# Two wide VectorE instructions per group of edges issued as four narrow ones each, in a graph kernel

## Chip, cores and metric

One NeuronCore of a Trainium2 chip runs the whole program. The metric is the device time in microseconds of one execution. Before the change it is 4437.84 us, the median of 3 runs (4432.64 to 4450.03).

## What is computed

Four layers work on a graph of 3125 nodes with 96 features and 100000 edges that are sorted by their target. Each layer normalizes its input, applies ReLU and adds its result to `x`. The change touches the last two layers:

```python
# message layer
msg  = relu(x[src] + edge_attr_96)                   # 100000 x 96
h    = x + segment_sum(msg, dst)                     # 3125 x 96
out  = x + relu(relu(h @ W1 + b1) @ W2 + b2)

# gate layer
edge_input = concatenate([x[src], edge_attr_32])     # 100000 x 128
messages   = gelu(edge_input @ mW1 + mb1) @ mW2 + mb2
gates      = sigmoid(gelu(edge_input @ gW1 + gb1) @ gW2 + gb2)
aggregated = segment_sum(messages * gates, dst)
update     = gelu(concatenate([x, aggregated]) @ uW1 + ub1) @ uW2 + ub2
out        = layernorm(x + update) * ln_g + ln_b
```

The two layers before them (a power iteration and three graph convolutions) use dense count matrices and are not touched.

## The kernel before

The edges are cut into 98 groups (`NG`) of 8 tiles (`GT`) of 128 edges, one edge on each partition. Both layers loop over these groups, and each engine has a queue of its own for the loop. Tables of node rows lie in HBM: `h_rows` (96 columns) for the message layer, `first_rows` (192 columns: the node's share of the message's and of the gate's first product) for the gate layer.

**Message layer.** POOL gathers the rows of a group by eight indirect DMAs of 128 rows (L777) into a ring of 7 slots (`RING`), after a wait that the slot's group is done (`group_done`, L774). SP loads the edges' features of the group into a second ring (L762). DVE then does, for each group, in this order: the add of rows and edges, 768 columns on 128 partitions, both inputs and the output in SBUF (L815, `added`); a one-hot matrix of edges against the 64 nodes of a step (L824, 512 columns); a wait for PE; the add of the step's sum to `aggT` (L828, 64 columns, one input in PSUM); and `group_done` (L829). ACT applies ReLU to the sum of rows and edges (L792), and PE multiplies rows by one-hot, 8 products into one PSUM tile (L865, `step_summed`). DVE waits for that sum before it goes on to the next group, so the steps of one group are a chain: L815, L792, L865, L828.

**Gate layer.** POOL gathers 192 columns a row (L981) into a ring of 7, after a wait for `rows_used`, which ACT raises with its second activation of the group (L1002). PE multiplies the edges' 32 features by the weights in two halves of four tiles (L1150, `edge_mixed`), and DVE adds each half from PSUM to the gathered rows (L1048, `added`). ACT applies Gelu to the gate's half (L999, into `gated`) and to the message's half (L1002, into `passed`). DVE multiplies `gated` by the gate's weights, which are one row broadcast over the 8 tiles, 768 columns with both inputs in SBUF (L1054, `weighed`), and sums each tile (L1057, `gate_sum`). ACT makes the gate from it (L1007). DVE makes the one-hot (L1078), scales it by the gate (L1080, `onehot_ready`), and adds the sum of the step before (L1064). PE sums (L1161). DVE's queue is written out over turns: the halves of group t (L1048), the product and sum of group t-1 (L1054, L1057), the one-hot of group t-2 (L1064, L1078, L1080).

The instructions of a group are unrolled; only the steps inside one group (99 in all for 98 groups) are a loop whose bounds are read from a table on the chip.

Of the kernel before, what the change touches and what calls it, by code (L numbers as in the profile page):

```python
# [6 lines left out]
D = 96  # L7
# [4 lines left out]
EP = 128  # L12
GT = 8
# [30 lines left out]
ALU = mybir.AluOpType  # L44
# [673 lines left out]
def message_layer(nc, g, src, dst, edges, w1, b1, w2, b2):  # L718

    with ExitStack() as ctx:  # L720
# [7 lines left out]
        rows = m.sb("rows", [EP, RING, GT, D], F32)  # L728
        edge = m.sb("edge", [EP, RING, GT, D], F32)
# [13 lines left out]
        added = m.sem("added"); sent = m.sem("sent"); group_done = m.sem("group_done")  # L743
# [60 lines left out]
        def _(dve):  # L804
# [6 lines left out]
            def add_edges(group):  # L811
                turn, r = divmod(group, RING)
                dve.wait_ge(edge_ready[r], 16 * (turn + 1))
                dve.wait_ge(rows_ready[r], 16 * GT * (turn + 1))
                nc.vector.tensor_tensor(rows[:, r, :, :], rows[:, r, :, :], edge[:, r, :, :],  # L815
                                        ALU.add).then_inc(added, 1)

            def sum_messages(group):
                begin, end, base = group_steps(nc, g, mybir.EngineType.DVE, group)
# [11 lines left out]
            for group in range(NG):  # L831
                add_edges(group)
                sum_messages(group)
# [49 lines left out]
def gated_layer(nc, g, src, dst, edges_T, mw1, mb1, mw2, mb2, gw1, gb1, gw2, gb2, uw1, ub1, uw2, ub2, ln_g, ln_b, out):  # L883
# [4 lines left out]
    with ExitStack() as ctx:  # L888
# [6 lines left out]
        rows = m.sb("rows", [EP, RING, GT, 2 * D], F32)  # L895
        onehot = m.sb("onehot", [EP, GT, SPAN], F32)
        table = nc.dram_tensor("first_rows", [N, 2 * D], F32, kind="Internal").ap()
        edge = m.sb("edge", [DE, 3, GT * EP], F32)
# [9 lines left out]
        gw2_sb = m.sb("gw2", [EP, D], F32)  # L908
# [116 lines left out]
        def _(dve):  # L1025
# [24 lines left out]
            def sum_gates(group):  # L1050

                values = gated[:, group % 2, :, :]
                dve.wait_ge(gate_in, group + 1)
                nc.vector.tensor_tensor(values, values, gw2_sb[:, :].unsqueeze(1).to_broadcast([EP, GT, D]),  # L1054
                                        ALU.mult).then_inc(weighed, 1)
                dve.wait_ge(weighed, group + 1)
                nc.vector.reduce_sum(gate[:, group % 3, :], values, AX).then_inc(gate_sum, 1)  # L1057

# [29 lines left out]
            for turn in range(NG + 2):  # L1088
                if turn < NG:
                    add_edges(turn)  # L1090
                if 0 < turn <= NG:
                    sum_gates(turn - 1)
                if turn > 1:
                    steps = sum_messages(turn - 2)
# [165 lines left out]
```

## Time and profile before

| what | us |
|---|---|
| median of 3 runs | 4437.84 |
| time of the profiled execution | 4435.82 |
| span of its profile, first to last instruction | 4433.7 |
| first gather of the message layer to its last one | 1811.9 to 2930.5 |
| first gather of the gate layer to its last one | 3042.3 to 4259.9 |
| busy over the span: PE / DVE / ACT / POOL | 2614.6 / 1728.5 / 575.6 / 1570.6 |

The profiled execution lies 2.0 us under the median, and 2.1 us of its time lie around the span. Busy time on POOL is the time in which an indirect DMA's descriptors are made; the transfer itself comes after it. A matmul's end in the trace is modelled. "issue" is idle time for which the profile shows no wait, and "remote" a wait whose releaser the profile can't name.

### The profile page before, as it was taken

Reading aid. Unit: us, or ns where it says so; the run is one execution under the profiler, and the core shown is the slowest. Engines: PE = TensorE matmul, PEld = TensorE weight load, DVE = VectorE, ACT = ScalarE, POOL = GpSimd, SP = SyncE. Lnnn points to the kernel's source line nnn. Section 1 sums busy time; section 2 is a strip of 40 time slices with the busy share of each in tenths; the row PEclk is TensorE's granted clock in tenths of the full one; section 3 lists DMA queues with packets and bytes.
Section 4 is the critical chain, followed back from the end, with each engine's and each line's share of the span. In section 5 each row is a group of like instructions: output and inputs, shape, how many; then the busy total and the mean of one; then the engine's idle time right before and its main releaser. Section 6 shows DMA issues by size and latency. Waiting matters only on the chain. (4 is left out here: it accounts for less than half of the span.)

```text
span 4433.7 us, 56784 instructions
## 1 busy us (share of the span) xinstructions
PE 2614.6 (59%) x17111; PEld 2043.8 (46%) x17112; DVE 1728.5 (39%) x3499; ACT 575.6 (13%) x943; POOL 1570.6 (35%) x1592
## 2 busy tenths in 40 slices
PE   5766666999997999122222222244457576676575
PEld 1111111899997777112222121233356565666572
DVE  6777777633335433211211111131234344444353
ACT  0112222400001300000000000010111111111110
POOL 0000000000000000566777776734656666666530
PEclk9667777799998899555555555555555555555555
DMA  0000000000000000222222222202222222222210
GB/s 22 0 0 0 0 0 0 3 2 2 2 2 1 4 1 1 80 62 65 73 70 78 64 67 62 71 25 83 71 70 75 74 71 73 76 72 74 71 41 11
DMA packets 98268, 179.56 MB, mean 40 GB/s; under 512 B 40771, under 2 KB 56440, under 8 KB 98074
## 3 DMA queue, kind: packets, MB, share of 16 engines
q0 software_dynamic: 62720, 115.71, 9.6%
q1 hardware_dynamic: 35354, 61.12, 4.5%
q8 instruction: 140, 2.29, 0.2%
q14 instruction: 54, 0.44, 0.0%
HBM read 171.91 MB, written 4.80 MB: 40 GB/s over the span
## 5 line engine op out<-in xcount | busy, mean ns | idle before, releaser
L981 POOL DMA_INDIRECT gate_rows<-first_rows,gate_src_i x784 | 767.2, 979 | 492.7 <-issue 271.0
L777 POOL DMA_INDIRECT msg_rows<-h_rows,msg_src_i x784 | 789.9, 1008 | 347.6 <-issue 233.1
L865 PE MATMUL msg_sums<-msg_onehot,msg_rows 128*96 128x64 f32 x1584 | 276.5, 369 | 876.0 <-DVE msg_onehot L824 561.0
L865 PEld LDWEIGHTS msg_sums<-msg_onehot,msg_rows 128*96 128x96 f32 x1584 | 260.8, 277 | 891.7 <-issue 891.7
L767 POOL IOTA msg_iota<- 128x3189 f32 x1 | 2.8, 2799 | 1785.3 <-POOLq L578 1785.3
L1150 PE MATMUL gate_sums<-gate_we,gate_edge 32*128 32x192 f32 x1568 | 554.4, 532 | 93.2 <-issue 70.7
L370 PE MATMUL cnt_sums<-dense_work 128*128 x1096 | 444.1, 499 | 202.8 <-DVE dense_work L319 151.5
L1150 PEld LDWEIGHTS gate_sums<-gate_we,gate_edge 32*128 32x128 f32 x1568 | 482.8, 326 | 123.5 <-issue 101.2
L510 PE MATMUL hop_sums<-dense_work,dense_counts 125*128 125x192 f16 x6250 | 522.4, 247 | 17.0 <-DVE dense_t L472 8.8
L510 PEld LDWEIGHTS hop_sums<-dense_work,dense_counts 125*128 125x128 f16 x6250 | 519.3, 98 | 19.9 <-DVE dense_t L472 9.6
L1161 PE MATMUL gate_sums<-gate_onehot,gate_passed 128*97 128x64 f32 x1584 | 284.6, 372 | 387.5 <-DVE gate_onehot L1080 355.1
L1161 PEld LDWEIGHTS gate_sums<-gate_onehot,gate_passed 128*97 128x97 f32 x1584 | 266.1, 282 | 436.9 <-DVE gate_onehot L1080 375.8
L319 DVE TENSOR_SCALAR dense_work<-dense_work,cnt_key,cnt_start_at 128x500 f16 x1096 | 400.2, 408 | 0.0
L828 DVE TENSOR_TENSOR msg_aggT<-msg_aggT,msg_sums 96x64 f32 x99 | 21.6, 218 | 893.5 <-remote 595.5
L370 PEld LDWEIGHTS cnt_sums<-dense_work 128*128 x1096 | 110.9, 101 | 526.4 <-issue 483.0
L1048 DVE TENSOR_TENSOR gate_rows<-gate_rows,gate_sums 128x768 f32<-128x768 f32 x196 | 183.7, 951 | 411.3 <-remote 217.2
L704 PE MATMUL conv_sums<-dense_work,dense_counts 125*128 125x288 bf16 x1875 | 236.4, 291 | 7.9 <-DVE dense_t L638 7.9
L315 DVE TENSOR_TENSOR dense_work<-dense_work 128x256 f16 x548 | 160.3, 292 | 195.6 <-issue 167.4
L999 ACT ACTIVATE gate_gated<-gate_rows 128x768 f32<-128x768 f32 x98 | 82.7, 844 | 1082.8 <-DVE gate_rows L1048 891.4
L792 ACT ACTIVATE msg_rows<-msg_rows 128x768 f32<-128x768 f32 x98 | 82.6, 843 | 1066.1 <-DVE msg_rows L815 819.0
L704 PEld LDWEIGHTS conv_sums<-dense_work,dense_counts 125*128 125x128 f16 x1875 | 186.1, 99 | 57.9 <-DVE dense_t L638 8.6
L472 DVE TENSOR_REDUCE dense_t<-hop_sums 125x384 f32<-125x768 f32 (+1 forms) x70 | 61.0, 871 | 327.6 <-PE hop_sums L510 327.6
(216 smaller groups left out, 2077.1 us busy)
## 6 DMA issues: line engine op xcount, KB each, us to landing
msg_edge<-edges SPq DMA_DIRECT2D x98, 384.0 KB
msg_rows<-h_rows,msg_src_i POOLq DMA_INDIRECT x784
gate_edge<-edges SPq DMA_DIRECT2D x98, 128.0 KB
gate_rows<-first_rows,gate_src_i POOLq DMA_INDIRECT x784
first_rows<-gate_first SPq DMA_DIRECT2D x6, 375.0 KB
all_x<-x SPq DMA_DIRECT2D x1, 1171.9 KB
h_rows<-all_h SPq DMA_DIRECT2D x1, 1171.9 KB
out<-all_x SPq DMA_DIRECT2D x1, 1171.9 KB
```

Of the source, the lines that this page charges most:

```text
L315: nc.vector.tensor_tensor(near[:, bass.ds(s & 1, 1), :].rearrange("p a (c i) -> p (a c) i", i=2), pairs2, src_n[:, bass.ds(tile, 2)].unsqu ...
L319: nc.vector.tensor_scalar(hot[:, bass.ds(s & 1, 1), i, 0:WIN * NT].rearrange("p a c -> p (a c)"), iota, key[:, bass.ds(tile + i, 1)], star ...
L370: end_of_pair = nc.tensor.matmul(sums[:, b, 0:WIN * NT], near[:, bass.ds(s & 1, 1), :].rearrange("p a (c i) -> p i (a c)", i=2)[:, i, :], ...
L510: last = nc.tensor.matmul(sums[:, g0 + i, 0:2 * D], counts[0:NP, at:at + 128], half[frm][:, k, :], start=(k == 0), stop=(k == NT - 1))
L704: last = nc.tensor.matmul(sums[:, 4 * (q % 2) + i, 0:3 * D], counts[0:NP, at:at + 128], parts[:, j, :], start=(j == 0), stop=(j == NT - 1))
L777: nc.gpsimd.indirect_dma_start(out=rows[:, r, k, :], out_offset=None, in_=table, in_offset=bass.IndirectOffsetOnAxis(ap=src_i[:, at:at + 1 ...
L865: last = nc.tensor.matmul(sums[0:D, 0, 0:SPAN], rows[:, group % RING, k, :], onehot[:, k, :], start=(k == 0), stop=(k == GT - 1))
L981: nc.gpsimd.indirect_dma_start(out=rows[:, r, k, :], out_offset=None, in_=table, in_offset=bass.IndirectOffsetOnAxis(ap=src_i[:, at:at + 1 ...
L999: nc.scalar.activation(gated[:, group % 2, :, :], r[:, :, D:2 * D], ACT.Gelu).then_inc(gate_in, 1)
L1048: nc.vector.tensor_tensor(to, to, products[:, :, 0:2 * D], ALU.add).then_inc(added, 1)
L1150: last = nc.tensor.matmul(sums[:, 2 * (part % 3) + k // 2, 256 * (k % 2):256 * (k % 2) + 2 * D], edge[:, group % 3, at:at + EP], we[:, :], ...
L1161: last = nc.tensor.matmul(sums[0:D + 1, 6, 0:SPAN], passed[:, group % 4, k, :], onehot[:, k, :], start=(k == 0), stop=(k == GT - 1))
```

## The change

One instruction of 768 columns becomes four of 192 columns (two tiles each), in two places: the add of rows and edges in the message layer, and the product with the gate's weights in the gate layer. The data, the order and the waits stay. The semaphore that the one instruction raised is raised by the last of the four. There is no wait between the four. In each layer 98 x 3 = 294 DVE instructions are added.

```diff
                 dve.wait_ge(rows_ready[r], 16 * GT * (turn + 1))
-                nc.vector.tensor_tensor(rows[:, r, :, :], rows[:, r, :, :], edge[:, r, :, :],
-                                        ALU.add).then_inc(added, 1)
+                for k in range(0, GT, 2):
+                    to = rows[:, r, k:k + 2, :]
+                    last = nc.vector.tensor_tensor(to, to, edge[:, r, k:k + 2, :], ALU.add)
+                last.then_inc(added, 1)
...
                 dve.wait_ge(gate_in, group + 1)
-                nc.vector.tensor_tensor(values, values, gw2_sb[:, :].unsqueeze(1).to_broadcast([EP, GT, D]),
-                                        ALU.mult).then_inc(weighed, 1)
+                for k in range(0, GT, 2):
+                    last = nc.vector.tensor_tensor(values[:, k:k + 2, :], values[:, k:k + 2, :],
+                                                   gw2_sb[:, :].unsqueeze(1).to_broadcast([EP, 2, D]), ALU.mult)
+                last.then_inc(weighed, 1)
```

## Rows read from the trace of the kernel before

**Rows 1.** Busy time by stretch: message loop, its tail, gate loop, its tail.
```profile
core 0: us, PE busy (x) PEld busy (x) DVE busy (x) ACT busy (x) POOL busy (x), PEclk, DMA share, GB/s
1793.00:2932.00 1139.00, 270.50 (x1550) 254.14 (x1548) 180.07 (x288) 84.25 (x103) 790.88 (x786) 0.50 0.25 70
3040.00:4280.00 1240.00, 777.88 (x2935) 702.21 (x2936) 486.58 (x643) 174.28 (x278) 767.16 (x784) 0.50 0.25 73
```
**Rows 2.** The gathers' lines: count, ns min/median/max, first and last start; then idle.
```profile
L777 POOL DMA_INDIRECT msg_rows<-h_rows,msg_src_i x784: 940/944/1727, 1811.9 to 2930.5; - x196
  issue: 233.1, 763
  DVEq L829: 96.6, 20
...
L981 POOL DMA_INDIRECT gate_rows<-first_rows,gate_src_i x784: 940/946/1694, 3042.3 to 4259.9; - x196
  issue: 271.0, 755
  ACT gate_passed L1002: 221.7, 29
```
**Rows 3.** DVE's waits in the message loop: us in total, times, longest.
```profile
DVE msg_aggT L828 <- remote: 595.5, 31, 41.0
DVE msg_rows L815 <- DMA msg_rows<-h_rows,msg_src_i: 11.4, 1, 11.4
```
**Rows 4.** Timeline, message layer: start, us, engine, line; POOL pauses, DVE released, gathers lengthened.
```profile
2295.63 0.94 POOL L777 DMA_INDIRECT msg_rows<-h_rows,msg_src_i  x1 [0.30 <-issue]
2302.33 0.22 DVE L828 TENSOR_TENSOR msg_aggT<-msg_aggT,msg_sums 96x64 f32 x1 [22.21 <-remote]
2302.77 0.96 DVE L815 TENSOR_TENSOR msg_rows<-msg_rows,msg_edge 128x768 f32<-128x768 f32 x1 [0.22 <-issue]
2302.87 1.67 POOL L777 DMA_INDIRECT msg_rows<-h_rows,msg_src_i  x1 [6.30 <-DVEq L829]
...
2304.85 0.94 POOL L777 DMA_INDIRECT msg_rows<-h_rows,msg_src_i  x1 [0.30 <-issue]
...
2308.45 0.96 DVE L815 TENSOR_TENSOR msg_rows<-msg_rows,msg_edge 128x768 f32<-128x768 f32 x1 [0.22 <-issue]
2308.59 1.64 POOL L777 DMA_INDIRECT msg_rows<-h_rows,msg_src_i  x1 [0.30 <-issue]
```
**Rows 5.** DVE instructions by length: ns min/median/max; two back to back in the gate layer.
```profile
L815 DVE TENSOR_TENSOR msg_rows<-msg_rows,msg_edge x98: 957/959/1027, 1823.5 to 2944.2; 128x768 f32<-128x768 f32 x98
L1054 DVE TENSOR_TENSOR gate_gated<-gate_gated,gate_gw x98: 943/951/993, 3065.4 to 4320.8; 128x768 f32<-128x768 f32 x98
L824 DVE TENSOR_TENSOR msg_onehot<-msg_iota,msg_dst_f x99: 691/693/744, 1824.8 to 2945.4; 128x512 f32<-128x512 f32 x99
L828 DVE TENSOR_TENSOR msg_aggT<-msg_aggT,msg_sums x99: 216/218/220, 1836.0 to 2949.5; 96x64 f32 x99
...
3622.63 1.81 DVE L1048 TENSOR_TENSOR gate_rows<-gate_rows,gate_sums 128x768 f32<-128x768 f32 x2
```
**Rows 6.** Timeline, gate layer: a gather during L1054, one during L1048.
```profile
3631.10 0.95 DVE L1048 TENSOR_TENSOR gate_rows<-gate_rows,gate_sums 128x768 f32<-128x768 f32 x1 [1.53 <-PE gate_sums L1150]
3631.30 0.94 POOL L981 DMA_INDIRECT gate_rows<-first_rows,gate_src_i  x1 [0.30 <-issue]
3631.97 0.95 DVE L1054 TENSOR_TENSOR gate_gated<-gate_gated,gate_gw 128x768 f32<-128x768 f32 x1
...
3632.55 1.19 POOL L981 DMA_INDIRECT gate_rows<-first_rows,gate_src_i  x1 [0.30 <-issue]
```
**Rows 7.** Timeline, gate layer: a gather that comes during L1078, with L1080 close behind.
```profile
3728.83 0.69 DVE L1078 TENSOR_TENSOR gate_onehot<-gate_iota,gate_dst_f 128x512 f32<-128x512 f32 x1
3729.15 1.19 POOL L981 DMA_INDIRECT gate_rows<-first_rows,gate_src_i  x1 [0.31 <-issue]
3729.56 0.69 DVE L1080 SCALAR_TENSOR_TENSOR gate_onehot<-gate_gate,gate_onehot 128x512 f32<-128x512 f32 x1
```
**Rows 8.** Timeline, end of the message loop, with POOL's last gather done.
```profile
2930.54 0.94 POOL L777 DMA_INDIRECT msg_rows<-h_rows,msg_src_i  x1 [0.30 <-issue]
...
2933.62 0.22 DVE L828 TENSOR_TENSOR msg_aggT<-msg_aggT,msg_sums 96x64 f32 x1 [3.46 <-PE msg_sums L865]
...
2939.31 0.22 DVE L828 TENSOR_TENSOR msg_aggT<-msg_aggT,msg_sums 96x64 f32 x1 [3.35 <-PE msg_sums L865]
...
2949.46 0.22 DVE L828 TENSOR_TENSOR msg_aggT<-msg_aggT,msg_sums 96x64 f32 x1 [3.36 <-PE msg_sums L865]
```
**Rows 9.** Timeline, gate layer: POOL's last gather before a pause, DVE's release, POOL's two returns.
```profile
3615.86 0.94 POOL L981 DMA_INDIRECT gate_rows<-first_rows,gate_src_i  x1 [0.30 <-issue]
3621.02 0.23 DVE L1064 SCALAR_TENSOR_TENSOR gate_aggT<-gate_sums,gate_aggT 97x64 f32 x1 [19.03 <-remote]
...
3625.23 0.83 ACT L1002 ACTIVATE gate_passed<-gate_rows 128x768 f32<-128x768 f32 x1
...
3626.32 0.94 POOL L981 DMA_INDIRECT gate_rows<-first_rows,gate_src_i  x1 [9.52 <-ACT gate_passed L1002]
...
3651.73 0.94 POOL L981 DMA_INDIRECT gate_rows<-first_rows,gate_src_i  x1 [5.39 <-ACT gate_passed L1002]
```
**Rows 10.** The queue that carries most engines' instructions: packets, MB, share.
```profile
q14 instruction: 54, 0.44, 0.0%
```

## Prediction

> **What bounds the kernel now.** I read first the busy time by stretch [rows 1]. In both loops that the change touches POOL is the busiest engine, 790.9 us of 1139 and 767.2 us of 1240, while DVE is busy for 180 and 487 us. TensorE is granted 0.50 of its clock in both, its lower level, and nothing in the change touches that. Then the lines of the gathers [rows 2]: a gather takes 0.944 us (median), the queue puts 0.30 us behind it ("issue" 233.1 us over 763 gaps), and so a group of eight costs POOL 8 x 1.25 = 10.0 us and 98 groups cost 980 us. What is left of POOL's time in the message layer is 96.6 us of waits for a free slot of the ring (20 times) and 790 - 784 x 0.944 = 50 us by which gathers last longer than the median. In the gate layer these two are 221.7 us and 767.2 - 784 x 0.944 = 27 us.
>
> Third, the timeline, for who lengthens a gather [rows 4, 6]. The gather at 2302.87 takes 1.67 us; L815 ran from 2302.77 to 2303.73. The one at 2308.59 takes 1.64 us; L815 ran until 2309.41. Both times the surplus is the rest of L815 less 0.12 to 0.13 us: the gather starts, wants something 0.12 us later, and gets it when L815 ends. The gather at 3632.55 takes 1.19 us beside L1054, which ended at 3632.92: 0.37 - 0.12 = 0.25 us surplus. The gather at 3631.30 lies wholly in L1048, which has one input in PSUM, and takes 0.94 us. So it is DVE instructions with two inputs in SBUF that hold POOL up. I paired each of the 784 gathers of a layer with the instruction that DVE runs 0.12 us after the gather's start. In the message layer 85 gathers meet L815 and lose 48.6 us in all; in the gate layer 57 meet L1054 and lose 16.2 us, and 97 meet L1078 or L1080 and lose 9.9 us. The sums agree with the 50 and 27 us above. The change reaches 48.6 + 16.2 = 64.8 us, 1.5% of the time.
>
> Fourth, the waits of DVE [rows 3], since they speak against POOL as the bound. DVE waits for gathered rows only once (11.4 us), but 595.5 us for a sum of PE's that the profile can't explain ("remote", 31 times, up to 41 us): the matmuls of that step are over in the trace long before. POOL in turn waits for DVE. At first sight DVE's chain is the bound and POOL has slack. But these long waits end when POOL pauses: POOL's gather at 2295.63 is its last before a pause (the ring is full), and DVE is released at 2302.33; in the gate layer the last gather starts at 3615.86 and DVE is released at 3621.02 [rows 4, 9]. Over both loops there are some 46 pauses like these. And once POOL has made its last gather, the message layer's remaining steps follow without one such wait, 5.7 us from one to the next [rows 8]. I don't know what delays the sums; I take it that it comes with POOL's running and ends with its pause, so that POOL's work, plus one pause for each filling of the ring, sets the length of the loop.
>
> **The change part by part.** *DVE's own time.* Lengths of 64, 512 and 768 columns take 218, 693 and 951 to 959 ns [rows 5]: about 1.04 ns a column and 0.15 us fixed. 192 columns should take 0.20 + 0.15 = 0.35 us. Two instructions of 768 columns without a wait between them take 1.81 us, not 1.90 [rows 5], so that 0.08 us of the fixed part overlap. Four of 192 columns take 4 x 0.35 - 3 x 0.08 = 1.16 us, against 0.95: 0.21 us more for a group, 41 us for 2 x 98 groups. Between the groups DVE waits for far more than that (idle over 950 us of the message loop), and a group's chain of 5.7 us becomes 5.9 us against POOL's 10.0 us. It is on the path only where POOL is done: the last 3 to 4 groups of the message layer [rows 8], and the first group of each loop. That is 5 x 0.21 = 1 us. The pauses of the gate layer end through L1064, L1078, L1080, L1048 and ACT, none of them changed; L1054 comes after them. If the cover were gone, all 41 us would show.
>
> *Gathers held up.* The trace shows no two instructions with both inputs in SBUF directly behind each other, so the cost is bounded from both sides. The low end: whenever one of the four ends, a waiting gather gets in. For this the nearest rows are L1078 and L1080 [rows 7]: the gather at 3729.15 has 1.19 us, a surplus of 0.25, which is the rest of L1078 (to 3729.52) less 0.12. L1080 starts 0.04 us later and needs the same thing, and the gather wasn't held by it. A gather then waits on average for half of 0.27 to 0.35 us, about 0.16 us. The four cover 1.16 of the 1.25 us between two gathers, so nearly every group of the message layer holds up one: 98 x 0.93 x 0.16 = 15 us, against 48.6. That saves 34 us. In the gate layer 57 of 98 become 57 x 1.16 / 0.95 = 70 at 0.16 us, 11 us against 16.2: 5 us saved. Together 39 us. The far ends: 64.8 us, if gathers fall between the instructions altogether; and, on the other side, the four hold POOL like one of 1.16 us. I take the first because of [rows 7], though there the two instructions are 0.04 us apart, while these overlap by 0.08 us in their records.
>
> The Trainium skill bears on this in two places. "SBUF — State Buffer", Who interferes with whom, says that a DVE instruction with two SBUF inputs contends with a GpSimd instruction that reads SBUF, and that the lock is exclusive and held for the whole instruction; by this rule, the trace agrees (1.67 us against 0.94 in [rows 4]). The same section infers, however, that making descriptors needs only the write interface, which such an add doesn't take; by that the change would give back nothing and cost the 1 us above, 4439 us. Here the rows speak against the inference. "Perfetto Trace Analysis", DVE / Act Engine Instruction, says that the next instruction may read only once the one before has finished executing, ahead of the end that the profiler reports; by that the overlap of 0.08 us in the records is no overlap of reads, and there is a gap for POOL.
>
> *Sum.* 4435.8 (the profiled execution) - 39 + 1 = 4397.8 us; the median lies 2.0 us above that execution, so 4400 us.
>
> *More instructions.* 294 more DVE instructions a loop, to 15 a group in the message layer now. Their code is loaded by the queue in [rows 10], 54 packets of 8 KB in all, 0.0% of the DMA engines. At nothing if it stays ahead; see the second rival.
>
> **The rivals.** *First, the four hold POOL as one.* If DVE's next instruction takes the second input's path before the waiting gather does, then a gather waits to the end of all four. Those that meet them lose 0.21 us more each: 85 x 0.21 + 57 x 0.21 = 30 us, and 1 us of tails: 4437.8 + 31 = 4469 us. It decides from the point at which the gap between two of the four is shorter than what POOL needs to get in. For it: the records overlap, and nothing in the trace shows such a pair. Against: [rows 7].
>
> *Second, the ring takes the gain back.* If the long waits for PE's sums have their own length, and POOL's pauses are only their result, a faster POOL only waits longer (96.6 and 221.7 us become more), and DVE's longer chain comes on top. The time is then between 4438 us (all hidden in DVE's waits) and 4437.8 + 98 x 0.21 = 4458 us (message layer in full, the gate layer's behind PE's products). For it: DVE hardly ever waits for rows [rows 3]. Against: the long waits end a few microseconds after POOL stops, POOL's pauses in the gate layer have the same two lengths, 9.5 and 5.4 us, again and again [rows 9], and none of those waits occurs once POOL is done [rows 8]. More code on DVE's queue would push the same way: 18 instead of 15 instructions a group, a fifth more loads of code, and if each brings a pause, 0.2 x 96.6 = 19 us.
>
> *Third*, only the message layer gains (34 us) and the gate layer, with its fixed rhythm of pauses, doesn't: 4405 us. I count it with the forecast.
>
> **How the numbers follow.** Forecast with the third case 0.53; the first rival 0.23; the second 0.24. A measurement of this kernel can tell about 0.5%, 22 us, from no change: below 4416 is faster, above 4460 slower. The forecast lies below 4416 but for a weak version of it (0.03). The second rival lies nearly all within 0.5%, with 0.04 beyond. So faster 0.51, same 0.22, slower 0.27. The range reaches from the full 64.8 us saved (4437.8 - 64.8 + 1 = 4374, of which I leave the last 4 us out) to the first rival's value: 4378 to 4470. The forecast's own range, by its bounds, is 4380 to 4415.
>
> **What the profile of the changed kernel would show.** In each layer 4 x 98 = 392 instructions of about 0.35 us in the place of the 98. The gathers' busy time: about 755 us in the message layer and 762 in the gate layer if the gathers get in; 808 and 780 by the first rival. The longest gather: about 1.3 us instead of 1.73, or over 1.9. POOL's waits: about 97 and 222 us by the forecast; by the second rival 130 and more in the message layer with gathers that did get shorter. What would make the prediction wrong: that the waits for the sums move with DVE's instructions rather than with POOL, since their 1000 us are not understood and a tenth of them is more than this gain.

## The result and the profile after

The changed kernel takes 4497.43 us (median of 4 runs, 4490.71 to 4501.32) beside 4438.1 us of the kernel before: ratio 1.0128, 95% interval [1.0105, 1.0152]. It is 59 us slower, where 38 us faster was forecast. The profiled execution took 4490.71 us, its span 4489.0. Later the same kernel before took 4428 to 4433 us in some groups of runs and 4059 to 4063 us in others, and in no profile taken beside the latter does one of the long unexplained waits occur (the kernel before itself was profiled only in the first runs). So each experiment is compared only with the runs of the kernel before beside it, and I call these the 4430 condition and the 4060 condition. The first runs are of the 4430 condition.

The busy time by stretch, of the message loop and the gate loop. The columns are those of [rows 1], and the stretches are the loops of this kernel, 16 and 29 us longer than there:

```profile
1793.00:2948.00 1155.00, 263.86 (x1511) 247.86 (x1509) 193.50 (x558) 81.95 (x100) 765.39 (x786) 0.50 0.28 69
3073.00:4342.00 1269.00, 787.95 (x2963) 707.17 (x2963) 509.49 (x928) 176.20 (x281) 758.90 (x784) 0.50 0.27 71
```

The lines of the gathers, of the add and (last) of the gate layer's gathers: ns min/median/max, first and last start.

```profile
L777 POOL DMA_INDIRECT msg_rows<-h_rows,msg_src_i x784: 943/947/1349, 1812.4 to 2946.8; - x196
L817 DVE TENSOR_TENSOR msg_rows<-msg_rows,msg_edge x392: 346/352/395, 1824.2 to 2979.6; 128x192 f32<-128x192 f32 x196
...
L983 POOL DMA_INDIRECT gate_rows<-first_rows,gate_src_i x784: 943/949/1445, 3073.3 to 4321.2; - x196
```

POOL is busy for less time than before in both loops (763.8 for 789.9 us in its gathers of the message layer, 758.9 for 767.2 in the gate layer), and the longest gather is down from the 1727 ns of [rows 2] to 1349. And yet both loops are longer. The waits say where it went: POOL's and then DVE's, in us in total, times, longest.

```profile
POOL gate_rows L983 <- ACT gate_passed L1004: 249.9, 32, 18.4
POOL msg_rows L777 <- DVEq L831: 141.9, 30, 11.3
```

```profile
DVE msg_aggT L830 <- remote: 692.0, 48, 27.0
DVE gate_aggT L1068 <- remote: 331.1, 38, 30.7
```

POOL's waits were 96.6 (20 times) and 221.7 (29) in [rows 2]. The late sums of the message layer are 48 for 31 in [rows 3]. They aren't all there, for where the trace lacks the record of PE's signal the same wait stands under "issue":

```profile
DVE msg_aggT L830 <- issue: 59.4, 6, 42.4
```

Whatever releaser is named, DVE's waits of over 4.5 us for a sum of this layer are 54 with 758 us, where they were 36 with 681 us, and the longest is as long as before (42.4 and 41.0 us). The timeline of the message layer shows one period of the new rhythm: start, us, engine, line.

```profile
2293.58 0.94 POOL L777 DMA_INDIRECT msg_rows<-h_rows,msg_src_i  x1 [0.30 <-issue]
2298.63 0.22 DVE L830 TENSOR_TENSOR msg_aggT<-msg_aggT,msg_sums 96x64 f32 x1 [19.10 <-remote]
2299.08 1.16 DVE L817 TENSOR_TENSOR msg_rows<-msg_rows,msg_edge 128x192 f32<-128x192 f32 x4 [0.23 <-issue]
2299.18 1.08 POOL L777 DMA_INDIRECT msg_rows<-h_rows,msg_src_i  x1 [4.65 <-DVEq L831]
...
2300.39 0.69 DVE L826 TENSOR_TENSOR msg_onehot<-msg_iota,msg_dst_f 128x512 f32<-128x512 f32 x1
2300.56 1.34 POOL L777 DMA_INDIRECT msg_rows<-h_rows,msg_src_i  x1 [0.30 <-issue]
...
2304.52 0.22 DVE L830 TENSOR_TENSOR msg_aggT<-msg_aggT,msg_sums 96x64 f32 x1 [3.44 <-PE msg_sums L867]
```

The four adds take 1.16 us. The gather that met the wide add took 1.67 us in [rows 4]; the one at 2299.18 takes 1.08. A new collision follows it: the gather at 2300.56 takes 1.34 us, held until L826 ends at 2301.08. Then a few groups pass quickly, a sum is late, POOL fills the ring and pauses, and the sum arrives. POOL pauses at every third group, for 4.1 to 4.8 us after the first time. Before, it paused 17 times in 98 groups, and five to ten groups passed from one run of late sums to the next.

I added up the idle gaps above 0.5 us between gathers ("pauses") and the other parts of each loop:

| us | before | after |
|---|---|---|
| message: first to last gather | 1119.6 | 1135.3 |
| of it gathers / pauses (count) | 789.9 / 96.3 (17) | 763.8 / 141.9 (30) |
| message: last gather to last sum | 18.2 | 36.8 |
| from there to the gate layer's first gather | 92.6 | 88.8 |
| gate: first to last gather | 1218.5 | 1248.8 |
| of it gathers / pauses (count) | 767.2 / 221.7 (29) | 758.9 / 263.1 (39) |
| gate: last gather to the loop's last sum | 77.6 | 71.6 |

The gathers give back 26.1 + 8.3 = 34 us, close to the forecast 39. The pauses take 45.6 + 41.4 = 87 us, and the message layer's end 19. Not all of this is the split's: further down, kernels with the wide add have a message loop nearly as long as this one (f3 and f4). The differences of the rows that aren't nested (15.7 + 18.6 - 3.8 + 30.3 - 6.0 us), with 0.5 us of a later start, make the 55 us by which the spans differ.

Two things about the late sums can be read from these traces. First, a pause isn't needed to end one. In the message loop before, 16 of the 31 end in a pause of POOL, and 15 with 230 us end while it gathers on, the longest among them:

```profile
1878.46 0.94 POOL L777 DMA_INDIRECT msg_rows<-h_rows,msg_src_i  x1 [0.30 <-issue]
1879.36 0.22 DVE L828 TENSOR_TENSOR msg_aggT<-msg_aggT,msg_sums 96x64 f32 x1 [41.02 <-remote]
1879.71 0.94 POOL L777 DMA_INDIRECT msg_rows<-h_rows,msg_src_i  x1 [0.30 <-issue]
```

Second, what is late is PE's signal and, as far as the trace tells, not its product. In the gate loop before, PE goes on with the next 16 products behind the sum that DVE waits for until 3621.02 ([rows 9]), and then stands idle:

```profile
3596.92 5.48 PE L1150 MATMUL gate_sums<-gate_we,gate_edge 32*128 32x192 f32 x16
3622.77 1.57 PE L1161 MATMUL gate_sums<-gate_onehot,gate_passed 128*97 128x64 f32 x8 [20.37 <-DVE gate_onehot L1080]
```

The trace has the updates of PE's semaphores too. The one for the sum comes at 3620.89, and those for the two halves of the 16 products at 3620.99 and 3621.08: 0.09 us apart, where the last products of the three had started at 3596.62, 3599.32 and 3601.88. The eight products of a half take 2.6 us, so halves that had themselves been held up couldn't have followed that closely. In 13 of the 16 waits of over 5 us for a sum in that loop (16 of 17 in the changed kernel) a second signal of PE's comes within 0.4 us of the release. In the split gate layer of the other condition (e2), and with the gathers thinned (g2), no wait of over 5 us for a sum occurs at all.

### The profile page after: what moved, and what is told of

It reads as the page before. It is cut to its first block and busy times, and to the rows that moved or that the text cites. A ratio compares the mean times of both kernels' runs of the same rounds, so it can differ in the third digit from the quotient of the medians.

```text
span 4489.0 us, 57372 instructions
## 1 busy us (share of the span) xinstructions
PE 2611.1 (58%) x17111; PEld 2036.1 (45%) x17112; DVE 1768.5 (39%) x4087; ACT 575.4 (13%) x943; POOL 1536.3 (34%) x1592
## 5 line engine op out<-in xcount | busy, mean ns | idle before, releaser
L983 POOL DMA_INDIRECT gate_rows<-first_rows,gate_src_i x784 | 758.9, 968 | 527.5 <-issue 277.5
L777 POOL DMA_INDIRECT msg_rows<-h_rows,msg_src_i x784 | 763.8, 974 | 389.3 <-issue 229.6
L1154 PE MATMUL gate_sums<-gate_we,gate_edge 32*128 32x192 f32 x1568 | 557.2, 533 | 96.6 <-issue 76.1
```

The lines of the kernel that those rows point to most:

```text
L777: nc.gpsimd.indirect_dma_start(out=rows[:, r, k, :], out_offset=None, in_=table, in_offset=bass.IndirectOffsetOnAxis(ap=src_i[:, at:at + 1 ...
L983: nc.gpsimd.indirect_dma_start(out=rows[:, r, k, :], out_offset=None, in_=table, in_offset=bass.IndirectOffsetOnAxis(ap=src_i[:, at:at + 1 ...
L1154: last = nc.tensor.matmul(sums[:, 2 * (part % 3) + k // 2, 256 * (k % 2):256 * (k % 2) + 2 * D], edge[:, group % 3, at:at + EP], we[:, :], ...
```

## Experiments in the 4060 condition

**Each half alone, and extra instructions.** The first four kernels ran together; the kernel before took 4063.25 us.

```diff
-                nc.vector.tensor_tensor(rows[:, r, :, :], rows[:, r, :, :], edge[:, r, :, :],
-                                        ALU.add).then_inc(added, 1)
+                for k in range(0, GT, 2):
+                    to = rows[:, r, k:k + 2, :]
+                    last = nc.vector.tensor_tensor(to, to, edge[:, r, k:k + 2, :], ALU.add)
+                last.then_inc(added, 1)
```

This is e1, the message layer's half.

> Only the message layer's add is issued as four instructions; the gate layer is as before. In the profile of the full change, gathers lost 26 us less to DVE in the message layer, yet POOL's pauses there went from 17 with 96 us to 30 with 142 us. Theory A (pace): the old instruction of 0.96 us held up one gather in four and so kept POOL at about 1.42 us a gather while DVE caught up; without that POOL runs at 1.25 us and PE's sums reach DVE late sooner. It expects the message layer's share of the loss, its loop and its tail: about +34 us, with about 30 pauses in the message layer and 29 in the gate layer. Theory B (code and chain): 3 more DVE instructions a group and 0.21 us more chain are the cost. It expects about half of the 59 us as well, +30 us. This run gives the split; it does not part A from B.

Measured 4060.5, ratio 0.9995 [0.9986, 1.0005]: no change. This expectation and the next three were written for a kernel before of 4438 us, so their sums of the loss have no counterpart here.

e2: the gate layer's half, the same edit on the product.

> Only the gate layer's product is issued as four instructions. Theory A (pace): fewer gathers are held up for long, and pauses of POOL go from 29 to about 39; +25 us. Theory B (code and chain): about half of the 59 us, +30 us. If the two halves do not add up to about 59 us, they act on each other.

Measured 4019.11, ratio 0.9895 [0.9879, 0.9912]: 44 us faster. A gain larger than the 16.2 us that L1054 costs in all by the prediction's pairing.

e3 puts three one-column instructions ahead of each wide one:

```diff
+                for i in range(3):
+                    nc.vector.memset(spare[:, i:i + 1], 0.0)
                 nc.vector.tensor_tensor(rows[:, r, :, :], rows[:, r, :, :], edge[:, r, :, :],
```

> The kernel before with three DVE memsets of one column (on a spare tile) put ahead of the one wide add and ahead of the one wide product of each group: as many DVE instructions as the changed kernel has, and about 0.2 us more on DVE's chain, but the wide two-input instructions and so POOL's hold-ups stay. Theory A (pace): within 10 us of the kernel before, pauses 17 and 29. Theory B (code and chain): about 4490 us like the changed kernel, with 30 and 39 pauses.

Measured 4063.36, ratio 1.0002 [0.9992, 1.0011]. The number of instructions costs nothing here.

e4 puts a one-column memset of POOL behind each gather, to slow their stream.

> The kernel before with a POOL memset of one column behind each gather, which slows POOL's own pace from 1.25 us a gather to some 1.4 to 1.5 us in all places, not only where DVE holds it up. Theory A (pace): the long unexplained waits of DVE for PE's sums shrink or go, and POOL's pauses with them; each loop becomes about 784 times the new spacing, at 1.45 us 1137 us: message layer +20 us, gate layer -80 us, in all about 4380 us. Theory B (code and chain), and the plain reading in which POOL is the bound: a slower POOL makes both loops longer, by up to 784 x 0.2 = 157 us each, and never shorter.

Measured 4064.31, ratio 1.0002 [0.9992, 1.0011]. The memset took 0.118 us and vanished in the 0.30 us between two gathers; their spacing stayed at 1.25 us. As a test of the pace it says nothing.

**The whole change**, the kernel before at 4062.62:

> The changed kernel itself once more, with its own runs of the kernel before beside it. In the four runs before this one the kernel before took 4063 us and had no long unexplained waits for PE's sums (in its first runs: 4438 us, with some 1000 us of them); there the message layer's part of the change gave nothing and the gate layer's part gave 44 us. If the kernel before takes about 4063 us again and the two parts add up, the changed kernel takes 4063 - 44 - 3 = 4016 us. If the kernel before takes about 4438 us, with the long waits, the changed kernel takes about 4497 us again, because the loss hangs on those waits. Theory B (3 more DVE instructions a group cost time by themselves) expects it slower than before in both cases.

Measured 4014.97, ratio 0.9881 [0.9864, 0.9897]: 48 us faster. What was 1.3% slower at first is 1.2% faster here. The waits of POOL and DVE in this run:

```profile
POOL gate_rows L983 <- issue: 278.5, 784, 39.8
POOL msg_rows L777 <- issue: 238.7, 783, 0.3
```

```profile
DVE gate_rows L1050 <- DMA gate_rows<-first_rows,gate_src_i: 441.6, 98, 17.3
DVE msg_rows L817 <- DMA msg_rows<-h_rows,msg_src_i: 426.9, 98, 11.4
```

DVE waits for rows in each of the 98 groups, POOL never pauses (its 39.8 us stand before the first gather of the gate layer), and no sum comes late. POOL is plainly the bound, and a gather that isn't held is time won.

**Slower gathers and two parts** ran beside a kernel before of 4059.42. The first has a POOL memset of 256 columns behind each gather:

```diff
                     ).then_inc(rows_ready[r], 16)
+                    if at >= 4:
+                        pool.wait_ge(spared, at - 3)
+                    nc.gpsimd.memset(spare[:, at % 4, :], 0.0).then_inc(spared, 1)
```

> The kernel before with a POOL memset of 256 columns behind each gather. The one-column memset tried earlier took 0.12 us and vanished in the 0.30 us between two gathers (spacing stayed 1.25 us); this one should take about 0.3 us and raise the spacing to 1.4 to 1.5 us. Where the kernel before takes 4063 us (POOL never pauses, DVE waits for rows): POOL is the bound there and each 0.1 us of spacing costs 784 x 2 x 0.1 = 157 us, so 4300 to 4450 us. Where it takes 4438 us: theory A (POOL at its full rate brings the long waits for PE's sums) expects fewer and shorter waits and a time within 30 us of before or below it; theory B (code and chain) expects 100 us or more on top.

Measured 4370.23, ratio 1.0767 [1.0749, 1.0785]. The spacing became 1.44 us; 2 x 784 x 0.19 = 298 us of the 311 are that.

> Both instructions issued as two of 384 columns instead of four of 192: one more instruction in each place and 0.07 us more on DVE's chain. Where before takes 4063 us: what counts is how the gathers fall against DVE's two-input instructions. If a waiting gather gets in whenever one of them ends, the product's hold-up falls from 0.20 to at most 0.1 us a group, but L1078 and L1080 move by only 0.07 us, so that most of the 42 us that L1080 costs stays: about 4050 us. If the gain came from narrow instructions alone, it would be half or more of the 48 us: 4040 us or less. Where before takes 4438 us: theory A expects a loss between 0 and 59 us, theory B about a third of it, 20 us.

Measured 4062.0, ratio 1.0009 [0.9999, 1.0019]. Two parts in both layers gain nothing; four gain 48 us, 44 of them in the gate layer.

**Why the gate layer gains more than its product cost.** The timeline of the gate layer with the wide product (e1), and with the split one (e2):

```profile
3491.47 0.95 DVE L1056 TENSOR_TENSOR gate_gated<-gate_gated,gate_gw 128x768 f32<-128x768 f32 x1
...
3492.07 1.17 POOL L983 DMA_INDIRECT gate_rows<-first_rows,gate_src_i  x1 [0.31 <-issue]
...
3493.55 0.95 POOL L983 DMA_INDIRECT gate_rows<-first_rows,gate_src_i  x1 [0.30 <-issue]
...
3494.69 0.69 DVE L1082 SCALAR_TENSOR_TENSOR gate_onehot<-gate_gate,gate_onehot 128x512 f32<-128x512 f32 x1
3494.80 1.40 POOL L983 DMA_INDIRECT gate_rows<-first_rows,gate_src_i  x1 [0.31 <-issue]
```

```profile
3500.16 1.16 DVE L1055 TENSOR_TENSOR gate_gated<-gate_gated,gate_gw 128x192 f32<-128x192 f32 x4
...
3500.78 1.09 POOL L981 DMA_INDIRECT gate_rows<-first_rows,gate_src_i  x1 [0.30 <-issue]
...
3502.18 0.95 POOL L981 DMA_INDIRECT gate_rows<-first_rows,gate_src_i  x1 [0.30 <-issue]
...
3502.86 0.69 DVE L1080 TENSOR_TENSOR gate_onehot<-gate_iota,gate_dst_f 128x512 f32<-128x512 f32 x1
3503.43 0.95 POOL L981 DMA_INDIRECT gate_rows<-first_rows,gate_src_i  x1 [0.30 <-issue]
```

In the first the product holds a gather, which is freed at the product's end (3492.42). From that moment the gathers have a fixed phase to DVE, and the next but one starts at 3494.80, inside the next wide two-input operation: 1.40 us. In the second the gather is freed at the end of the third quarter, 0.27 us ahead of the product's end. The next but one then comes that much earlier against what follows the product, near the end of the operation before it, and takes 0.95 us. This repeats in nearly every group: with the wide product the operation that answers to L1080 holds 91 gathers for 41.7 us in all and the product 96 for 19.8; with the split one 0.1 and 12.1 us. With halves (e7) the gather is freed at the end of the second half, the product's own end, so the phase is the old one: the operation held 84 gathers for 38.4 us. So some 36 of the 44 us are phase and 8 the shorter holds.

I tried to make the phase without the split by one more reduce behind the product's reduce:

> The kernel before, all wide instructions kept, with one DVE reduce of 96 columns with a single input ahead of L1064, L1078 and L1080 in the gate layer, so that these come about 0.17 us later, nearly as after the split. Where before takes 4063 us: in the message-only run L1080 held up 91 of 98 groups' gathers for 41.7 us in all and the product for 19.8 us; after the gate split L1080 held up one, L1078 5 us, the product 12 us. If most of the gain is this shift of the later instructions and not the narrow product, this run gains 30 us or more: 4033 us or less. If the gain is the narrow product itself, it gains nothing: 4063 us. Where before takes 4438 us: theory A gives a loss of some 10 us at most or none, theory B about 10 us (one instruction more in 98 groups).

Measured 4058.37, ratio 0.9997 [0.9988, 1.0007]. The added 0.24 us ran inside a wait for ACT that was there before, and nothing behind it moved; the test was badly placed. The next one moves the reduce itself:

```diff
                                         ALU.mult).then_inc(weighed, 1)
+                nc.vector.reduce_sum(spare[:, group, :], gw2_sb[:, :].unsqueeze(1).to_broadcast([EP, 2, D]), AX)
                 dve.wait_ge(weighed, group + 1)
```

> The kernel before with its wide gate product (one instruction of 768 columns) and, between that product and its reduce, one more VectorE reduce of 192 columns over a resident table, whose result nobody uses. It moves the reduce, the sum that follows and the two wide two-input operations at the group's end some 0.2 to 0.3 us later behind a product that stays wide. Phase theory (most of the gain of the split gate product is that a later gather no longer falls on the wide operation L1080 of before, 41.7 us of hold-up over 91 gathers): L1080's counterpart holds under 8 us, the product still about 20 us, gate gathers about 765 to 772 us in all, time 4020 to 4030 where the kernel before takes about 4062 (ratio about 0.991). Rival (the split product itself lets the gathers in, and nothing else matters): hold-ups unchanged at about 60 us, gate gathers 805, time 4062 (ratio 1.000). If the kernel before takes about 4438 here, with its long waits for sums, a theory that pace brings those on says ratio above 1.00, one that the number of instructions does says the same.

Its runs fell in the 4430 condition (before 4428.46), where it took 4428.75, ratio 0.9998 [0.9984, 1.0012]. That the phase makes the gain is therefore read from the timelines and from e7, and wasn't tested by itself.

## Experiments in the 4430 condition

**Extra instructions**, as e3, beside the same runs:

> The kernel before with three one-column VectorE memsets ahead of each wide add and each wide product: the instruction count of the split without its shorter holds. Where the kernel before takes about 4062: both theories say no change, 4063. Where it takes about 4438: that the pace of the gathers brings on the late sums says about 4438 with 46 to 49 pauses of POOL in the two loops; that the longer instruction stream does says about 4490 with over 60 pauses.

Measured 4452.78, ratio 1.0057 [1.0041, 1.0073]. Neither of the two expected patterns. POOL's waits:

```profile
POOL gate_rows L985 <- ACT gate_passed L1006: 223.5, 29, 15.9
POOL msg_rows L778 <- DVEq L832: 128.6, 29, 9.6
```

The gate layer is as before, and the message layer has the changed kernel's pauses, without its narrow adds. The reason is in the gathers: its line reads 764.1 us, as after the change and not as before (789.9). The memsets move the wide add to where few gathers meet it: it holds only 14 gathers, for 6.4 us in all, where it held 85 for 48.6 before. Of the loss of 24 us (11 between the two profiled executions) the message layer has the most: the first gather to the last sum takes 20 us more than before in the message layer (1158.0 for 1137.8) and 7 us less in the gate layer.

**The whole, its halves, and a delay.** Four kernels, the kernel before at 4430.55.

> The whole change again. If the kernel before takes about 4430 here: 4485, ratio 1.013, 30 pauses of POOL in the message layer and about 39 in the gate layer. If it takes about 4062: 4015, ratio 0.988, no pauses. That the ratio depends on the condition of the chip and not on the day says both; if the loss of the first runs was a matter of chance, the ratio is below 1.00 in either.

Measured 4501.67, ratio 1.0151 [1.0122, 1.0179]. The loss is repeatable and comes with the condition. The pauses are 30 and 36.

> The add of the message layer split alone, the gate layer as before. Where the kernel before takes about 4430: if the message layer carries its share of the loss, 30 pauses there, its end some 15 to 35 us later, total 4450 to 4465 (ratio 1.005 to 1.008); if the two layers only lose together, ratio 1.000 or below. Where it takes about 4062: 4060.

Measured 4439.36, ratio 1.0001 [0.9981, 1.0021]: the 30 pauses are there, the loss isn't.

> The product of the gate layer split alone, the message layer as before. Where the kernel before takes about 4430: if the gate layer loses by its own split, its loop is some 30 us longer with 38 to 40 pauses instead of 29, total 4450 to 4465; if it loses only because it follows a changed message layer, ratio 1.000. Where it takes about 4062: 4019.

Measured 4483.84, ratio 1.0115 [1.0081, 1.0149]. More than was expected, and most of the loss: 53 us of the 71 that the whole change loses beside the same runs. POOL's waits of f2 and then of f3:

```profile
POOL gate_rows L983 <- ACT gate_passed L1004: 187.3, 29, 17.1
POOL msg_rows L777 <- DVEq L831: 139.3, 30, 11.8
```

```profile
POOL gate_rows L981 <- ACT gate_passed L1002: 234.0, 30, 18.1
POOL msg_rows L777 <- DVEq L829: 107.4, 16, 11.7
```

With all idle gaps above 0.5 us, f3's gate loop has 43 pauses of 257 us in 1241.0, and f2's 34 of 198 in 1199.4.

f4 has one reduce of 192 columns behind the wide add of the message layer:

> The kernel before with one VectorE reduce of 192 columns over a resident table behind the wide add of each group of the message layer (result unused): one instruction and some 0.25 us more to a group, no split. Where the kernel before takes about 4430: that a slower step of VectorE brings the late sums sooner says 30 pauses and gathers held less (764 us), as with the three memsets, and a total about 4450; that the number of instructions does (one here, three there) says 17 to 20 pauses and 4430 to 4435. Where it takes about 4062: no change.

Measured 4439.57, ratio 1.0027 [1.0001, 1.0053]; 17 pauses, gathers 784.2 us. A slower step of DVE (0.25 us a group) doesn't bring the sums late more often; with e9 in the gate layer (30 pauses) that holds for both layers.

The four profiles ran side by side, so their loops can be compared better than with the first profile. A loop is taken from its first gather to its last sum, in us:

| kernel (add, product) | message loop | gate loop | gate: gathers, pauses |
|---|---|---|---|
| f4 (wide, wide; delay) | 1165.9 | 1264.5 | 773.0, 199.4 |
| f2 (split, wide) | 1176.6 | 1270.5 | 772.9, 198.2 |
| f3 (wide, split) | 1167.5 | 1308.8 | 758.2, 257.3 |
| f1 (split, split) | 1170.3 | 1333.2 | 757.8, 269.8 |
| first runs: before (wide, wide) | 1137.8 | 1296.1 | 767.2, 221.7 |
| first runs: after (split, split) | 1172.1 | 1320.4 | 758.9, 263.1 |

Among the four, splitting the product makes the gate loop 44 us longer (f3 against f4) and 63 us (f1 against f2): the gathers give back 15 us and the pauses take 58 and 72. Splitting the add moves the message loop by 11 us at most. So the 34 us by which the message loop grew from the first profile before to the one after are mostly not the split's: kernels with the wide add have 28 to 30 of them. With unchanged instructions a loop's length varies by some 30 us from one profile to another (the message loop in f3, the gate loop in f4), so one profile each doesn't give the share of a layer.

**Two parts, slower gathers, a shorter ring.** The kernel before at 4432.64.

> Add and product in two instructions of 384 columns. Where the kernel before takes about 4430: if the loss grows with the number of places at which a gather can get in, 4440 to 4470 (ratio 1.003 to 1.009) and 34 to 40 pauses in the gate layer; if only four parts shift the rhythm, as where the kernel before takes 4060, ratio 1.000 and 29 to 34 pauses.

Measured 4487.64, ratio 1.0132 [1.0106, 1.0159], above the range expected. Two parts lose about as much as four (55 us; 59 and 71).

> The kernel before with a 256-column memset of POOL behind each gather, which made the gathers 1.44 us apart and cost 311 us where POOL bounds the loops (ratio 1.077). Where the kernel before takes about 4430: if the late sums come from the density of the gathers, they and the pauses (46 in the two loops) get fewer and the time grows by far less than 311 us, 4430 to 4550; if they are fixed by something else, the time grows by 311 us less what the pauses leave as slack, 4600 to 4740.

Measured **4370.1**, ratio 0.9869 [0.9847, 0.9892]. POOL made slower by 0.19 us a gather makes the kernel 62 us faster. It is the time that the same kernel took in the other condition (4370.23, e6). Its waits are of the other condition too:

```profile
DVE msg_rows L820 <- DMA msg_rows<-h_rows,msg_src_i: 646.8, 98, 12.8
DVE gate_rows L1058 <- DMA gate_rows<-first_rows,gate_src_i: 616.2, 98, 18.9
...
DVE msg_aggT L833 <- PE msg_sums L870: 319.1, 95, 3.7
```

No sum is late, where the kernel before has hundreds of microseconds of "remote".

```diff
-RING = 7
+RING = 6
```

> Six row buffers instead of seven, in both layers. Where the kernel before takes about 4430: if each late sum lasts until POOL has filled the ring and pauses, each is some 10 us shorter (8 gathers), the pauses are more in number (over 55 in the two loops) and the time is longer if a pause has a price of its own, 4450 to 4520; if the late sums do not depend on POOL's pauses, their longest stays at about 41 us. Where it takes about 4060: no pauses, 4060 to 4070.

Measured 4419.29, ratio 0.9977 [0.9962, 0.9993]. The two loops have 18 + 32 = 50 pauses, and the longest wait for a sum in the message layer is 41.2 us. Neither followed the ring, and the time is a little shorter: that a late sum has to last until the ring is full, as I had read [rows 4, 9], isn't borne out by its length, nor by the 15 late sums above that end without a pause.

**A spacing between, with the whole change.** The kernel before at 4433.49; the memset has 160 columns.

> The whole change with a POOL memset of 160 columns behind each gather. From 0.118 us for one column and 0.33 for 256 an estimate of 0.25 us each, of which about 0.14 lie in the gap between two gathers: spacing about 1.36 us. If the density of the gathers makes the late sums and 1.36 is thin enough: no pauses, and 4015 (the change where POOL bounds) + 1568 x 0.11 = about 4187 in either condition, ratio about 0.945 against a kernel before at 4430. If the split loses by something else, pauses stay and the time is 4400 or more. If the bound of the density lies above 1.36: pauses in part of the loops, 4250 to 4450.

Measured 4381.37, ratio 0.9875 [0.9838, 0.9912]. The gathers are 1.36 us apart. POOL's waits for a free slot, and DVE's for the message layer's sums:

```profile
POOL gate_rows L990 <- ACT gate_passed L1014: 88.7, 19, 7.9
...
POOL msg_rows L779 <- DVEq L836: 23.9, 8, 3.9
```

```profile
DVE msg_aggT L835 <- remote: 707.2, 58, 29.8
```

That is in the range of the third case. The late sums of the message layer are still there (692 us in the changed kernel without the memsets), those of the gate layer are down from 331 to 252 us, and the pauses of the two loops from 405 to 39.5 + 101.7 = 141 us. If the limit is the same for both kernels, it lies above 1.36 and, by g2, at 1.44 or below.

**What orders all of them.** For each profile of the 4430 condition I took the mean time from one gather's start to the next, gaps over 0.8 us left out, beside the pauses of that layer:

| kernel | message: spacing, pauses, us | gate: spacing, pauses, us |
|---|---|---|
| before | 1.314, 17, 96 | 1.284, 29, 222 |
| e9 (shift in the gate layer) | 1.313, 18, 99 | 1.286, 30, 230 |
| e10 (three memsets in both) | 1.282, 30, 129 | 1.291, 30, 225 |
| f4 (delay in the message layer) | 1.306, 17, 113 | 1.292, 33, 199 |
| g3 (ring of 6) | 1.308, 18, 117 | 1.297, 32, 195 |
| f2 (message split) | 1.280, 30, 139 | 1.292, 34, 198 |
| f3 (gate split) | 1.310, 16, 107 | 1.274, 43, 257 |
| g1 (halves in both) | 1.277, 29, 143 | 1.278, 34, 255 |
| f1 (the change again) | 1.278, 30, 141 | 1.272, 36, 270 |
| after | 1.280, 30, 142 | 1.274, 39, 263 |
| h (change, 160 columns) | 1.394, 23, 40 | 1.380, 25, 102 |
| g2 (before, 256 columns) | 1.507, 1, 0.5 | 1.470, 0, 0 |

In this table the pauses go with the density of the gathers and not with the form of DVE's instruction: e10 has the wide add and the split's pauses, f4 an extra instruction and the pauses of before. Without the memsets of g2 and h, though, the median spacing is 1.25 us in every row, and the means differ only by how long DVE holds gathers up. So the other rows don't tell cause from effect, since a group that runs without a late sum is also where gathers get held. g2 and h do better, for they set the spacing from outside.

## Why the prediction was wrong

**Right.** Four instructions of 192 columns take 1.16 us, 0.35 each. A waiting gather gets in between two of them: the add holds gathers for 8.6 us in all (15 forecast, 48.6 before), the product for 1.9 (11 forecast). The first rival, four holding POOL as one, is out: 763.8 us of gathers in the message layer where it wanted 808. DVE's longer chain costs nothing by itself (e3, and within noise f4).

**A term mis-sized.** The message layer's gathers came to 763.8 instead of 755 us, because the shift brings L826 onto a gather: 37 gathers held for 13.1 us, 1.1 us before. I had kept the holds of the other instructions as they were, and each freed gather moves all that follow it. In the gate layer the same effect, at the 4060 condition, made the gain 44 us where 5 were forecast.

**The step that failed** is the one behind [rows 3, 4 and 9]: "that POOL's work, plus one pause for each filling of the ring, sets the length of the loop", with the number of pauses kept. The pauses weren't a fixed price. They went from 17 and 29 to 30 and 39 and took 87 us, against 34 us that the gathers gave back; in the gate layer alone, where the loss is, they took 58 us for 15 (f3 against f4). Nor does a pause end each late sum: I had read that from the episodes of [rows 4, 9], and 15 of the 31 in [rows 3] end while POOL gathers. Of the two halves of the sentence before, that the late sums come with POOL's running was borne out by g2, and that they end with its pause was not. The second rival named this kind of result (POOL's waits of 130 us and more in the message layer, with shorter gathers; it shows 141.9) and priced it at most at 4458 us, since it let the gain be lost but not more than lost. That a supply which runs faster made its consumer late more often fits every profile, but isn't shown for the split itself. I had also written that the waits aren't understood and that a tenth of them outweighs the gain; that sentence deserved more than 0.24, and a range above 4470. The chances have a slip besides: 0.53 less 0.03 is 0.50 for faster and leaves 0.23 for same, not 0.51 and 0.22.

**Shown and not shown.** Shown: the loss repeats (f1), is mostly the gate layer's (f3 against f2 and f4), is not made by one instruction more or a slower step (e9, f4) nor, in the gate layer, by three more (e10), and the late sums vanish when POOL's stream is thinned to 1.44 us (g2), while at 1.36 us most of them stay and cost less (h). Shown for the 4060 condition: the same change gains 1.2%. Only argued: that the split loses because its gathers are denser; every profile agrees, and no run split the product while holding the density as it was. For the message layer of e10, with three instructions more and 30 pauses, the same is argued. Open: what in the chip delays PE's signals, why a density of 1.25 us does it in one condition and not in the other, and what sets the condition; chip number 13 stands under runs of both (e6 to e8 and g1 to g3). That the thinning works by time and not by the memset's own writes and waits wasn't separated either, and the 19 us at the end of the message loop (36.8 us for 18.2) aren't the split's alone: f3 and f4, whose adds are wide, show 39.0 and 35.4 us there too.

No version is best in both conditions. The whole change is best at 4060 (4015). The two thinned kernels are best at 4430 (4370 and 4381). The one with 256 columns costs 7.7% at 4060 (e6), and the one with 160 wasn't run there.

## What to carry to other kernels

When a profile holds large waits that it can't name, a small gain elsewhere isn't safe at any size: count how often such a wait begins and what it is worth (here 46 pauses at 7 us), and ask what the change does to that number, before adding up microseconds saved. When two engines take turns at a shared path, an instruction that ends a hold earlier moves all later meetings by that amount; look at what the next two operations of the waiting engine will then meet. And repeat the comparison on other days or chips if the baseline has such waits: the sign of this change depends on it.

## What the runs showed of the hardware

- A gather's descriptor work that meets a DVE instruction with two SBUF inputs waits for the end of that one instruction, even among back-to-back ones: 1.09 us in the third of four (e2), 1.17 us beside a whole one (e1), 1.67 us where the gather starts 0.10 us after the whole one does [rows 4].
- The same kernel takes 4059 to 4063 or 4428 to 4438 us. All but a few us of the difference lie in the two loops in which POOL gathers (1137.8 and 1296.1 us before, 992.7 in e2 and 1069.7 in e1 for the same instructions); with gathers 1.44 us apart it is gone (4370.2 and 4370.1).
- A POOL memset of one column takes 0.118 us, of 160 columns 0.248, of 256 0.328, and some 0.14 us of it fit between two gathers at no cost.
- In the 4430 condition DVE waits up to 42.4 us for a sum of PE's, where some 3.4 us are usual. PE's signals are late and come in bunches, 0.09 us apart, for products whose starts lie 2.6 to 2.7 us apart. Thinning the gathers from 1.25 to 1.36 us leaves waits of up to 29.8 us, thinning to 1.44 none over 3.7.
